# Moving a small variance calculation from VectorE to GpSimd in the first stage of a normalise, filter and spectral kernel

## The reference, cut to what matters

```
x = x + filtered_lrelu(groupnorm(x), f)        # first stage of the kernel
x = x + spectral_conv(groupnorm(x), a, b, c, d) # the other two stages
groupnorm(v): groups of 4 channels; (v - mean) / sqrt(var + 1e-5)
```

## Time and profile before

| | |
|---|---|
| median of 3 runs | 5329.47 us (5323.57 to 5330.88) |
| the profiled execution: its time, its span | 5320.26 us, 5318.5 us |
| granted TensorE clock over the span | 0.986 |
| `phase1` | from 0 to about 2850 us |
| `phase2`, `phase3` | the rest |

### The profile page before, as it was taken

How to read it: one execution, slowest core, us unless ns; L and a number is a source line. 1 busy time by engine, 2 the same in 40 slices (tenths; PEclk the granted TensorE clock), 3 DMA queues, 4 the chain that set the end, 5 groups by cost and what they waited for, 6 DMA issues and landing times. The chain is left out here.

```text
span 5318.5 us, 209180 instructions
## 1 busy us (share of the span) xinstructions
PE 4860.2 (91%) x83744; PEld 4306.2 (81%) x83744; DVE 4204.8 (79%) x6501; ACT 3399.4 (64%) x6422; POOL 2563.8 (48%) x2566
## 2 busy tenths in 40 slices
PE   8999999999999999999997698998988988988999
PEld 6887888887878888888886588888888888888999
DVE  7888888888888888888886888888888888883333
ACT  6767767767677677676673566666666666663332
POOL 6757757757567577576672233333333333330000
PEclk9999999999999999999997799999999999999999
DMA  1131131131321321322314122222222222227999
GB/s 53 53 106 53 53 109 54 49 109 53 88 71 53 98 61 53 100 59 71 91 49 148 48 63 79 78 64 79 71 71 79 66 76 79 63 79 293 420 421 398
DMA packets 606620, 553.42 MB, mean 104 GB/s; under 512 B 14900, under 2 KB 540084, under 8 KB 589364
## 3 DMA queue, kind: packets, MB, share of 16 engines
q1 hardware_dynamic: 606132, 546.48, 31.2%
HBM read 277.99 MB, written 268.44 MB: 103 GB/s over the span
## 5 line engine op out<-in xcount | busy, mean ns | idle before, releaser
L1203 DVE TENSOR_TENSOR Ml<-ring,Mh 128x1024 f16<-128x1024 f32 x1024 | 1198.9, 1218 | 201.0 <-ACT Mh L1170 193.2
L246 POOL TENSOR_TENSOR Y<-Yf,Y 128x532 f16<-128x532 f32 x1024 | 1212.0, 1196 | 156.0 <-ACT Y L501 113.8
L1170 ACT ACTIVATE Mh<-ring 128x1024 f16<-128x1024 f32 x1024 | 986.4, 1022 | 301.8 <-PE ring L1104 301.2
L1104 PE MATMUL ring<-wcur,b_hi 64*128 64x128 f16 x16384 | 748.1, 217 | 177.4 <-DVE Ml L1203 138.2
L1104 PEld LDWEIGHTS ring<-wcur,b_hi 64*128 64x128 f16 x16384 | 609.7, 94 | 248.0 <-DVE Ml L1203 155.9
L280 PE MATMUL ring<-uth,A 128*128 128x266 f16 x6144 | 789.5, 277 | 18.1 <-issue 17.0
L677 DVE TENSOR_TENSOR Yf<-ring,L 128x532 f32<-128x532 f32 x1024 | 686.5, 707 | 108.1 <-ACT L L497 93.1
L280 PEld LDWEIGHTS ring<-uth,A 128*128 128x128 f16 x6144 | 598.6, 98 | 154.0 <-issue 19.3
L1104 PE MATMUL ring<-wcur,b_lo 64*128 64x128 f16 x8192 | 715.6, 216 | 0.0
L497 ACT ACTIVATE L<-ring 128x532 f32<-128x532 f32 x1024 | 600.8, 604 | 37.3 <-PE ring L280 27.9
L286 PE MATMUL ring<-ut,g 128*128 128x266 f32 x2048 | 570.6, 401 | 3.1 <-POOL g L227 3.0
(11 more groups left out here) (138 smaller groups left out, 9678.8 us busy)
## 6 DMA issues: line engine op xcount, KB each, us to landing
xb<-in_x SPq DMA_DIRECT2D x128, 512.0 KB, 4.2
x<-x1b SPq DMA_DIRECT2D x64, 1024.0 KB, 6.8
spec<-sp_out SPq DMA_DIRECT2D x256, 256.0 KB, 3.5
xin<-spec SPq DMA_DIRECT2D x128, 512.0 KB, 6.6
fd<-ft SPq DMA_DIRECT2D x128, 512.0 KB, 4.0
F<-fd SPq DMA_DIRECT2D x64, 1024.0 KB, 20.1
xq<-x SPq DMA_DIRECT2D x64, 1024.0 KB, 16.9
out<-yq SPq DMA_DIRECT2D x64, 1024.0 KB, 18.6
```

What stands on the lines that cost most here:

```text
L246: pool.tensor_tensor(Y[:, e, 1, m], Yf[:, m], Y[:, e, 0, m], ALU.subtract).then_inc(e_yl, 1)
L1104: mm = pe.matmul(ring[:, UNIT_PAIR[n], t, 128 * k:128 * k + 128], b[r, z, 4 * u + k, :], wcur[r, z, w, :], start=(part == 0), stop=(part = ...
L1170: act.activation(hi, ps, ACT.Copy).then_inc(e_hi, 1)
L1203: dve.tensor_tensor(lo, ps, hi, ALU.subtract).then_inc(e_lo, 1)
```

## The change

The variance leaves DVE. [...] POOL calls it in the statistics step, behind the `Yt` tail and ahead of high 2. ACT's root takes a doubled variance and scales it by a half. `nmr` is also made on POOL, ahead of `ground`, as half the sum times the reciprocal, and `ground` subtracts it instead of adding it. DVE keeps the pair sums and the reciprocal, and its `stats_copy` waits until POOL has used the sums of the half before.

```diff
 # POOL
 def ground(q, k, half):
     if k % HALF == 0:
+        par = k // HALF % 2
+        pool.wait_ge(k_rs, half + 1)
+        carry(pool, carried[0])
+        pool.tensor_tensor(nmr[:, par, :], hm[:], rstd[:, par, :], ALU.mult).then_inc(k_nm, 1)
         pool.wait_ge(k_nm, half + 1)
...
-                       ALU.mult, ALU.add).then_inc(g_ok, 1)
+                       ALU.mult, ALU.subtract).then_inc(g_ok, 1)
+
+def variance(h):
+    pool.wait_ge(k_tot, h + 1)
+    carry(pool, carried[0])
+    pool.tensor_scalar(hm[:], tot[:, 0], 0.5, None, ALU.mult).then_inc(k_m2, 1)
+    pool.tensor_scalar(e2[:], tot[:, 1], 1.0 / 256, None, ALU.mult).then_inc(k_m2, 1)
+    pool.wait_ge(k_m2, 5 * h + 2)
+    pool.tensor_tensor(sq[:], tot[:, 0], hm[:], ALU.mult).then_inc(k_m2, 1)
+    pool.tensor_tensor(e2[:], e2[:], tot[:, 2], ALU.add).then_inc(k_m2, 1)
+    pool.wait_ge(k_m2, 5 * h + 4)
+    pool.tensor_tensor(var[:], e2[:], sq[:], ALU.subtract).then_inc(k_m2, 1)
+    pool.wait_ge(k_m2, 5 * h + 5)
+    carry(pool, carried[0])
+    pool.tensor_scalar(var[:], var[:], 0.0, 2 * EPS, ALU.max, ALU.add).then_inc(k_var, 1)
...
     pool.tensor_tensor(Yt[:, e, 1, :], ...)         # the Yt tail
+    if half is not None and k % HALF == 2:
+        variance(half)
     high(2)
...
 # ACT, root
-    act.activation(std[:], var[:], ACT.Sqrt).then_inc(k_sd, 1)
+    act.activation(std[:], var[:], ACT.Sqrt, scale=0.5).then_inc(k_sd, 1)
 # DVE
 def stats_copy(h, pr):
     dve.wait_ge(p_st, h + 1)
+    wait(dve, k_nm, h)
...
-def stats_var(h): ...                               # four instructions
...
     dve.reciprocal(rstd[:, par, :], std[:]).then_inc(k_rs, 1)
-    dve.wait_ge(k_rs, h + 1)
-    dve.scalar_tensor_tensor(out=nmr[:, par, :], ...).then_inc(k_nm, 1)
...
-        if k % HALF == 2:
-            stats_var(half)
```

More of the change, by code:

```diff
@@ L109, in phase1 @@
         e2 = sb("e2", [128, HALF])
+        hm = sb("hm", [128, HALF])
         sq = sb("sq", [128, HALF])
@@ L260, in first @@
                 pool.wait_ge(c_ld, 16 * len(ld_consts))
+                variance(0)
                 ground(0, 0, 0)
@@ L600, in stats_copy @@
                                   ).then_inc(k_tot, 1)
[L602 to L611, removed]
             def stats_out(h, par):
@@ L617, in stats_out @@
                 dve.reciprocal(rstd[:, par, :], std[:]).then_inc(k_rs, 1)
-                dve.wait_ge(k_rs, h + 1)
-                dve.scalar_tensor_tensor(out=nmr[:, par, :], in0=tot[:, 0], scalar=-0.5, in1=rstd[:, par, :],
-                                         op0=ALU.mult, op1=ALU.mult).then_inc(k_nm, 1)
             def batch_in(b):
@@ L776, in first @@
                 stats_copy(0, 0)
-                stats_var(0)
                 stats_out(0, 0)
```

## The result

The changed kernel takes 5289.9 us (median of 4 runs, 5282.6 to 5294.3) against 5328.7 us for the kernel before (4 runs). The ratio is 0.9929, 95% interval 0.9917 to 0.9942, so it is faster by 0.7%, or 38.8 us. The granted TensorE clock is 0.985 over the span, against 0.986 before, so the clock doesn't explain the gain. The prediction was 5270 us, with a range of 5247 to 5318: the direction is right, and some 20 of the 59 us expected are missing.

What follows compares the result with a forecast made beforehand. TensorE was taken to lead, busy 91% of the span. Of 1.21 us a half, 0.95 was kept: 63 times, 60 us, less about 1 in the prologue, so 5270 us against the median of 5329.5; range 5247 to 5318.

Steps and rivals of the forecast that it cites:

- one such wait: TensorE's weight loads waiting for another engine, at `A`: 54 times, once per half, 0.78 us each, 42.1 us in all.
- The two gaps: TensorE's gaps in the step behind the variance: 0.78 us for `A`, and 0.53 us more ahead of the `Yb` products.
- The two variance instructions: Last two variance instructions on VectorE, four elements per partition: their 1170 and 1122 ns were mostly waiting for GpSimd.
- 1.21 us a half: Step behind the variance, 10.81 against 9.60 us: both gaps can close, 63 times, 76 us at most.
- The price of a small GpSimd instruction: GpSimd's variance: 0.25 us per one-input, 0.15 per two-input instruction, 0.07 per wait on itself, 1.41 us together.
- D: How much later GpSimd's high 2, and all behind it, comes in the statistics step: 0.77 us (0.16 to 1.33).
- 1.12: Lateness in us that low 3 could have before TensorE waits for it in `down_rows`.
- `ground` costs 0.77 us: End of GpSimd's statistics step: with `ground` at 0.77 us, GpSimd is 0.6 us late, made good within the next step.
- `Yc` is harmless or 0.4 us late: `Yc` behind the variance: no loss if `ground` still runs at its issue, otherwise up to 0.41 us late beneath high 0.
- Rival (a): VectorE's reciprocal also waits for GpSimd's running product: 0.5 to 1.05 us a half left, 5265 to 5300 us; chance 0.15.
- Rival (b): Stops behind the loop's edge swallow the saving in 31 of 63 halves: 39 us gained, 5291 us; chance 0.17.
- Rival (c): Small GpSimd instructions averaging 0.46 us make low 3 late and eat the gain; up to 5392 us; chance 0.08.

Runs made afterwards that it cites:

- e5: The changed kernel with the sign moved so `ground` multiplies and adds, plus VectorE issuing `Yc` ahead of `Yf` 0 and 1: 5201.4 us, ratio 0.9778.
- e8: The kernel before, with VectorE issuing `Yc` ahead of `Yf` 0 and 1 and nothing else changed: 5246.5 us, ratio 0.9841.
- e3: The kernel before with the four variance instructions left on VectorE but called directly behind `stats_copy`, ahead of `a_low` 0: 5284.6 us, ratio 0.9931.
- e1: The changed kernel with the sign moved (minus half the sum), so that `ground` multiplies and adds again: 5244.6 us, ratio 0.9853.
- e2: The kernel before with `nmr` of opposite sign, still made on VectorE, and `ground` multiplying and subtracting: 5316.9 us, ratio 0.9988.
- e7: The changed kernel without `nmr`; `ground` subtracts the mean first, then multiplies by the reciprocal: 5256.2 us, ratio 0.9876.
- e4: The changed kernel with `ground` adding, plus six 128x4 GpSimd instructions ahead of the variance, writing scratch nobody reads: 5303.8 us.

## Why the prediction was right, and what was mis-sized

- *The list shows one such wait, for `A`.* Misread: TensorE's longer wait for `Yc` (65.4 us, 138 times) stood in the same list. The timeline led the forecast to the part of it behind the variance, as its second gap; the part in the ordinary steps (84 of the 138) was left out, and e5 and e8 go for it. The two gaps were also said to make up the 1.21 us; they add up to 0.78 + 0.53 = 1.31, and the loads between them took 1.52 instead of 1.61 us.
- *The two variance instructions were waiting for GpSimd.* Right. The earlier trace rows read so, and e3 shows it: 0.16 and 0.17 us with GpSimd idle.
- *1.21 us a half, 76 us at most.* Nearly right: e1 has the change with `ground` as quick as before, and gains 78 us, 1.28 us a half by the steps.
- *The price of a small GpSimd instruction.* Forecast 0.25 and 0.15 us, measured 0.23 and 0.20 us. From `Yt`'s end at 1030.80 to high 2's start at 1032.40 pass 1.60 us, for a forecast of 1.41. The waits on GpSimd's own results were too cheap in part: I had 0.07 us each, and two of them leave 0.08, but 0.20 us pass idle ahead of the last one and 0.30 us behind `nmr`, where the code has a further semaphore instruction (`carry`) behind the wait. High 2 follows `Yf` 2's end at 1031.27 by 1.13 us, where it was 0.17 before: D is 0.96, for a forecast of 0.77, and still under 1.12. TensorE doesn't wait for low 3.
- *`ground` costs 0.77 us, and GpSimd's lateness is made good within the step.* This is the step that failed. I listed that `ground` now subtracts, and never priced it: I took the operation to be free and the duration from the earlier trace rows. It took 2.08 us, and 2.16 in the statistics step. At the end of that step GpSimd has no room for 1.3 us more, and the gap ahead of `up_rows` grew from 0.22 to 1.00 us in the step behind it, 0.78 us or 49 of the 76 us. e1 and e2 show it from both sides. e7 shows that subtract first and multiply second is as slow.
- *`Yc` is harmless or 0.4 us late.* It came out better: it ran in 0.22 us beneath `ground`, and ordinary steps gained 0.08 us. That gave back some of what `ground` took. e2 has this alone: 5.5 us faster (0.1%), within what I called no change. The forecast let `Yc` wait for `ground`'s end. e8 shows that wait for the quick form; behind the variance `Yc` escaped it by luck, being issued 0.13 us into `ground`.
- *Rival (a), the reciprocal waits too.* Falls: it took 0.17 us at 1033.73, beneath a product that ran from 1033.12 to 1034.31, and the same in 63 halves. The Trainium skill (SBUF — State Buffer, "Who interferes with whom") leaves it out of its list; the trace agrees.
- *Rival (b), the loop edge takes half back.* Falls: the stops behind the edges add up to 15.0 us in the changed kernel and 14.9 before. e1 gains 1.28 us a half by the steps away from the edges, 81 us in all, and the medians differ by 78. That the edges can take something shows in e2, 10 us. The stops of the earlier trace rows lie 40 loads into the new step, 12 of `up_cols` and 28 of `down_rows`, where the forecast counted 28.
- *Rival (c), GpSimd becomes late.* Its mechanism is real and stands at the place worked out, as e4 shows; but six small instructions weren't enough for it. GpSimd did become late, through another instruction and at another place, and not by so much that the gain was lost.
- *The number.* That it lay only 20 us off is luck in part. The sum left 0.95 us a half. By the steps, 0.26 that I gave up for `Yc` and the edges was not needed, the two gaps gave 0.07 more (1.28), and two ordinary steps gave 0.16 that I had not foreseen; `ground` took 0.78. That makes 0.66 us a half, 42 us in 63 halves, for 38.8 measured. With nothing but `ground`'s price put in, the forecast would have been 59 - 49 = 10 us.

Not settled: why the pairs with a subtraction are slow on GpSimd. The runs show three pairs at one size and one kind of operand, and nothing of what the engine does inside. Open, too, is what sets the length of the stops behind the loop's edges.

## What to carry to other kernels

Read the duration of a tiny instruction against its neighbours on the other engine: here 1.17 us for four elements was a wait, and it went away either by moving the instruction to the other engine or by issuing it where that engine is idle, though in e3 another instruction fell beneath in its place. When an edit swaps an operation inside an unchanged GpSimd instruction, price the new form by a run and not by the old row: here the new form cost 40 us, as much as the change gained on the whole. And look for gaps in the steps that repeat: an order swap of one 0.2 us instruction (e5 against e1) was worth 0.75%, another 40 us.

## What the runs showed of the hardware that was not expected

- GpSimd's `tensor_scalar` on 128x512 float32 with two pointer scalars takes 0.77 us as multiply and add, 2.08 us as multiply and subtract, and 2.08 us as subtract and multiply.
- Two-input VectorE instructions wait beneath GpSimd's cast (0.63 us) and its products (1.18 us). Beneath `ground` it depends on the moment: `Yc` issued up to 0.14 us into it ran in 0.22 us (60 times in e1, 60 in the changed kernel); issued 0.15 to 0.65 us into it, it ended some 0.85 us behind `ground`'s start, whether `ground` took 0.77 us (65 times in e8) or 2.08 us (60 times in e7); and issued 1.1 us or more into the slow form, up to its last tenths, it ran in 0.22 us again.
- A dependent pair of small GpSimd instructions (0.20 to 0.24 us each) has an idle time of 0.08 us between them where there is only a wait, as behind the cast (0.07 us), and of 0.20 and 0.30 us in the two places where the code has a `carry` behind the wait.
